# Probabilities of query blocks 8 to 14 transposed through DRAM and VectorE instead of TensorE

## The reference

```
energy = (x @ Wq) @ (x @ Wk).T          # per batch, 2048 x 2048
energy = where(pad | causal, -inf, energy)
z = softmax(energy / sqrt(32)) @ (x @ Wv)
```

## Time and profile before

| | |
|---|---|
| time, median of 3 runs | 1645.36 us (1645.16 to 1645.95) |
| the profiled execution: its time, its span | 1649.54 us, 1647.7 us |
| busy: PE, DVE, ACT, POOL | 98%, 53%, 35%, 22% of the span |
| mean granted TensorE clock | 0.994 of 2.4 GHz |
| transposes of probabilities on TensorE (L970) | 272, of which 168 are of blocks 8 to 14 in both batches |
| DMA | 130.87 MB, 79 GB/s on average |

### The profile page before, as it was taken

How to read it: one execution, slowest core, us unless ns; L and a number is a source line. 1 busy time by engine, 2 the same in 40 slices (tenths; PEclk the granted TensorE clock), 3 DMA queues, 4 the chain that set the end, 5 groups by cost and what they waited for, 6 DMA issues and landing times.

```text
span 1647.7 us, 20596 instructions
## 1 busy us (share of the span) xinstructions
PE 1610.7 (98%) x7538; PEld 1323.5 (80%) x7538; DVE 876.6 (53%) x1784; ACT 572.6 (35%) x990; POOL 363.9 (22%) x562
## 2 busy tenths in 40 slices
PE   8999999999999999899999899999999999999999
PEld 6887888877788888677777688888888888888887
DVE  6757544477664444688888966333333332423311
ACT  5432121134222212466666544232323232333322
POOL 1212100022220000288888911000000000000000
PEclk9999999999999999799999999999999999999999
DMA  6302110131221104456664354111212111121100
GB/s 213 101 27 96 45 52 26 39 110 58 72 74 34 52 26 142 135 140 171 157 178 163 112 157 126 64 39 56 47 52 50 54 39 64 39 64 32 46 0 26
DMA packets 177161, 130.87 MB, mean 79 GB/s; under 512 B 121073, under 2 KB 121073, under 8 KB 176907
## 3 DMA queue, kind: packets, MB, share of 16 engines
q1 hardware_dynamic: 175264, 126.10, 25.9%
q10 hardware_dynamic: 1797, 3.46, 0.6%
HBM read 87.34 MB, written 42.18 MB: 79 GB/s over the span
## 4 chain that ended last, share of the span: by engine, by line
PE 85%; DVE 6%; ACT 4%; issue 2%; POOL 2%; DMA 0%; DVEq 0%; SPq 0%; ACTq 0%; POOLq 0%
PE banks L760 82%; PE banks L970 2%; ACT plain L1318 2%; DVE split L1697 1%; ACT split L1154 1%; PE banks L770 1%; DVE plain L2068 1%; ACT plain L1328 1%; DVE tile_x L2075 0%; DVE plain L2058 0%; DMA plain<-in_L_xattn_Wk 0%; POOL split L1572 0%; DVE plain L1836 0%; DVE split_q L1697 0%; POOL split L1579 0%
## 5 line engine op out<-in xcount | busy, mean ns | idle before, releaser
L760 PE MATMUL banks<-split_q,split 128*128 128x512 f32 x2328 | 565.8, 393 | 4.9 <-POOL split L1572 3.0
L760 PE MATMUL banks<-split 128*128 128x512 f32 (+5 forms) x2304 | 543.0, 385 | 8.3 <-DVE split L1697 5.9
L760 PEld LDWEIGHTS banks<-split_q,split 128*128 128x128 f32 x2328 | 434.1, 188 | 98.7 <-POOL split L1572 4.0
L760 PEld LDWEIGHTS banks<-split 128*128 128x128 f32 (+3 forms) x2304 | 414.8, 185 | 103.9 <-issue 8.2
L760 PE MATMUL banks<-split,split_q 128*128 128x512 f32 (+3 forms) x1728 | 393.2, 380 | 7.2 <-DVE split_q L1697 4.1
L760 PEld LDWEIGHTS banks<-split,split_q 128*128 128x128 f32 x1728 | 308.4, 189 | 60.3 <-DVE split_q L1697 4.9
L2216 DVE TENSOR_TENSOR split<-plain,split 128x512 fp32r<-128x512 f32 x128 | 88.5, 692 | 386.8 <-ACT split L1473 386.7
L1467 ACT ACTIVATE plain<-banks,small 128x512 f32<-128x512 f32 x128 | 88.3, 690 | 402.4 <-PE banks L760 402.4
L1697 DVE TENSOR_TENSOR split<-banks,split 128x512 fp32r<-128x512 f32 (+5 forms) x232 | 146.1, 637 | 149.4 <-ACT split L1154 149.1
L1154 ACT ACTIVATE split<-banks 128x512 fp32r<-128x512 f32 (+5 forms) x232 | 124.0, 555 | 244.5 <-PE banks L970 190.9
L1506 POOL TENSOR_TENSOR small<-small 128x1 f32<-128x1 f32 x64 | 13.1, 204 | 475.6 <-DVE small L1733 475.4
(11 more groups left out here) (157 smaller groups left out, 1265.3 us busy)
## 6 DMA issues: line engine op xcount, KB each, us to landing
plain<-in_x SPq DMA_DIRECT2D x64, 256.0 KB, 2.7
xo_scratch<-plain SPq DMA_DIRECT2D x32, 256.0 KB, 2.3
x_scratch<-plain SPq DMA_DIRECT2D x32, 256.0 KB, 2.0
plain<-x_scratch SPq DMA_DIRECT2D x32, 256.0 KB, 3.0
tile_x<-xo_scratch SPq DMA_DIRECT2D x32, 256.0 KB, 3.2
xg_scratch<-tile_x SPq DMA_DIRECT2D x32, 256.0 KB, 2.1
out<-plain SPq DMA_DIRECT2D x32, 256.0 KB, 2.1
plain<-xg_scratch SPq DMA_DIRECT2D x7, 1024.0 KB, 5.5
```

The lines of the kernel that those rows point to most:

```text
L760: mm = nc.tensor.matmul(out, left(c, l), right(c, r), start=start and c == 0 and (l, r) == PASSES[0], stop=stop and c == chunks - 1 and (l ...
```

## The change

Blocks 8 to 14 are `turned`. When X(i) is done, SP stores the row of probabilities to `p_dram`, chunk by chunk (`store_p`). Each chunk is then loaded back into the same place of `Srow` by four DMAs (`load_p`), so that the 32x32 squares of every 128x128 tile stand where the transposed tile wants them. SP issues the loads of chunks 0 and 2. A new step O(i) has ScalarE issue those of chunks 1 and 3, after a wait for the store of the same chunk. A new step I(i,c) has VectorE wait for the four loads and transpose the chunk in 32x32 squares into bank 2 or 3; TensorE has no part in T of these blocks. The list of steps is another one for these blocks.

```
+        if turned(i) and n1 > n0:
+            g = i // 4 + 1
+            order += [("Q", g, 0), end[0], ("Q", g, 1), end[1], ("I", i, 0), ("I", i, 1), ("Q", g, 2), ("T", i, 0),
+                      ("Q", g, 3), ("T", i, 1), ("V", i, 0), ("I", i, 2), ("S", i + 1, 0), ("T", i, 2)]
+            order += [("S", i + 1, c) for c in range(1, n1)]
+            order += [("X", i + 1, 0), ("O", i + 1, 0), ("V", i, 1), ("V", i, 2)]
+        elif turned(i):
+            order += [end[0], ("S", i + 1, 0), ("S", i + 1, 1), ("I", i, 0), ("T", i, 0), ("S", i + 1, 2), ("I", i, 1),
+                      ("T", i, 1), end[1]]
+            order += [("S", i + 1, 3)] if n0 > 3 else []
+            order += [("X", i + 1, 0), ("I", i, 2), ("V", i, 0), ("T", i, 2), ("O", i + 1, 0)]
+            order += [("I", i, 3), ("V", i, 1), ("T", i, 3)] if n0 > 3 else [("V", i, 1)]
+            order += [("V", i, c) for c in range(2, n0)]
...
-            order += [("S", i + 1, n0), ("X", i + 1, 0)]
+            order += [("S", i + 1, n0), ("X", i + 1, 0), ("O", i + 1, 0)]
...
+        def load_p(eng, b, i, c):
+            at, w = c * 512, width_of(i, c)
+            eng.wait_ge(p_out[c], squares_in(b, i, c) * 16)
+            squares_of = p_dram[c, 0:P * w].rearrange("(q s c i r) -> i s c q r", q=QB, s=32, i=QB, r=32)
+            for n in range(QB):
+                eng.dma_start(Srow[32 * n:32 * n + 32, i % 2, at:at + w].rearrange(
+                    "p (c q r) -> p c q r", q=QB, r=32), squares_of[n]).then_inc(p_in[c], 16)
...
+                def store_p(i, c):
+                    n, at, w = squares_in(b, i, c), c * 512, width_of(i, c)
+                    if n > 1:
+                        sp.wait_ge(p_in[c], (n - 1) * QB * 16)
+                    sp.dma_start(p_dram[c, 0:P * w].rearrange("(p n) -> p n", n=w), Srow[:, i % 2, at:at + w]).then_inc(p_out[c], 16)
...
                     sp.dma_start(x1_dram[b * S + i * P:b * S + (i + 1) * P, :], U[:, i % 2]).then_inc(
                         x1_out[i % 2], 16)
+                    if turned(i + 2):
+                        sp.wait_ge(p_ready, b * NB + i + 2 + 1)
+                        for c in range(chunks_of(i + 2)):
+                            store_p(i + 2, c)
+                        for c in range(0, chunks_of(i + 2), 2):
+                            load_p(sp, b, i + 2, c)
...
-                    elif kind == "T":
+                    elif kind == "T" and not turned(i):
...
+                    elif kind == "O" and turned(i):
+                        for n in range(1, chunks_of(i), 2):
+                            load_p(act, b, i, n)
...
+                    elif kind == "I":
+                        n, at, w = TURNS["p", b, i, c], c * 512, width_of(i, c)
+                        dve.wait_ge(p_in[c], squares_in(b, i, c) * QB * 16)
+                        dve.wait_ge(tp_free, n + 1)
+                        nc.vector.transpose(PS[:, 2 + n % 2, 0:w], Srow[:, i % 2, at:at + w]).then_inc(tp_full, 1)
```

More of the change, by code:

```diff
@@ L89, with turned, squares_in @@
 T_BEFORE = [sum(chunks_of(j) for j in range(i)) for i in range(NB + 1)]
+def turned(i):
+    return 8 <= i < NB - 1
+def squares_in(b, i, c):
+    return sum(turned(j) and c < chunks_of(j) for j in range(NB)) * b + sum(
+        turned(j) and c < chunks_of(j) for j in range(i + 1))
 def attention_order(b):
@@ L109, in attention_order @@
         end = [(kind, i - 1, 0) for kind in "AB"]
-        if n1 > n0:
+        if turned(i) and n1 > n0:
[11 more added lines that the diff above has]
+            order += [("V", i, c) for c in range(2, n0)]
+        elif n1 > n0:
             g = i // 4 + 1
@@ L169, in turns_of_attention @@
         for kind, i, c in ORDERS[b]:
-            if kind == "T":
+            if kind == ("I" if turned(i) else "T"):
                 order.append(("p", b, i, c))
@@ L255, in build @@
         xg_dram = nc.dram_tensor("xg_scratch", (B * S, E), F32, kind="Internal").ap()
+        p_dram = nc.dram_tensor("p_scratch", (C, P * 512), F32, kind="Internal").ap()
         h_dram = nc.dram_tensor("h_scratch", (TILE, E), F32, kind="Internal").ap()
@@ L438, in build @@
         h_out, hb_in = sem("h_out"), sem("hb_in")
+        p_out, p_in = [sem(f"p_out_{c}") for c in range(C)], [sem(f"p_in_{c}") for c in range(C)]
         block = ctx.enter_context(nc.Block())
@@ L966, in _ @@
                             pe.wait_ge(p_ready, b * NB + i + 1)
+                        if c == 0 and turned(i - 1):
+                            pe.wait_ge(tp_full, n)
                         pe.wait_ge(tp_free, n + 1)
```

## The result

The changed kernel takes 1685.4 us (median of 4 runs, 1684.0 to 1691.1) where the kernel before takes 1645.7: ratio 1.0237, 95% interval 1.0209 to 1.0265. It is 39.7 us slower; 33.7 were forecast, and the time lies in the range. The profiled execution's span is 1689.3 us against 1647.7, 41.6 us more.

A forecast was written before the change was run, and what follows sets the result against it. TensorE, busy for 98% of the span, was taken to bound the kernel. Saved transposes, waits and low clock summed to -19.7 + 47.8 + 5.6 = +33.7 us, a median of 1679 us, range 1654 to 1698.

The forecast's parts named there:

- What is taken away: TensorE's transposes in blocks 8 to 14: 168 tiles in two batches at 0.118 us, 19.7 us saved.
- The walk: Steps followed through stretches 8 to 14: TensorE waits before V, 23.9 us a batch, 47.8 in two.
- the slower pace of two queues: SP and ScalarE loading at once: ScalarE's eight issues take up to 1.3 us more, 5 us over four stretches; upper end only.
- The clock: TensorE's clock falls behind the 4.4 to 4.7 us gaps in four stretches, 1.4 us each: 5.6 us.
- The sum: Whole kernel: -19.7 + 47.8 + 5.6 = +33.7 us, median 1679 us.
- The first (O doesn't hold ScalarE): Load issues on ScalarE slip past its other work or take next to nothing: +9.9 us, 1655; chance 0.14.
- The second (every stretch pays for the clock): More gaps in changed stretches cost clock, 19.6 us, and the two queues crowd, 5: +52.7 us, 1698; chance 0.14.
- The third (hand-overs stay ahead): ScalarE and VectorE stay ahead of TensorE, so the 168 tiles are simply saved: 1625.7 us; chance 0.07.
- the loads are not late: Loads by squares in the changed stretches could land 6 us later without a price.

The follow-up runs named there:

- experiment 10: Changed kernel with only blocks 12 to 14 turned, I and T of chunks 0 and 1 a step earlier, B behind X, O last: 1637.5 us, 0.9941 of before.
- experiment 1: Changed kernel with only step O(i+1) moved behind T(i,3) in four-chunk stretches: 1656.7 us, 1.0065 of the kernel before.
- experiment 3: Changed kernel with O in its place but reduced to its waits for the stores, SP issuing every load: 1661.0 us, 1.0091 of before.
- experiment 2: Changed kernel with all loads issued by SP and none by ScalarE: 1661.2 us, 1.0089 of the kernel before.
- experiment 4: Changed kernel with O issuing only the four loads of chunk 1, SP the rest: 1670.3 us, 1.0144 of the kernel before.
- experiment 9: Changed kernel with I and T of chunks 0 and 1 a step earlier, B behind X, O still ahead of T(i,3): 1675.6 us, 1.0182 of before.

## Why the prediction was right

**What is taken away.** Forecast 0.118 us a tile. Experiment 10 gives 0.11. From the start of V(7,0) to T(15,0) of the first batch takes 146.3 us before and 150.4 in experiment 1, +4.2, with 13.0 us of waits; so 84 tiles saved 8.8 there, 0.105 each. In experiment 10 the same time is 4.9 and 4.7 us shorter than before in the two batches, 9.6 in all. The term was 19.7 and is 17.6 by the first of these, 18.8 by the median of experiment 10 and 19.2 by its trace: right, or slightly high.

**The walk.** The places were right in all seven stretches, and the sum, 23.9 a batch, came out as 25.3. The wait before the last V of stretches 12 and 13 was under-sized: 5.1 and 6.3 for 4.4 and 4.7. ScalarE reached its first issue 2.8 us after X (2.7 forecast), but the eight issues, put at 5.2 us, took 5.57 in stretch 12 and 6.50 in stretch 13, and 5.56 and 5.60 in those of the second batch. The term was too small by 0.4 us, and in one stretch by 1.3. These are ScalarE's issues in stretch 13 of the first and of the second batch, and SP's in stretch 13 of experiment 3 (ns least/median/most):

```profile
L527 ACTq DMA_DIRECT2D plain<-p_scratch x8: 564/651/1543, 326.3 to 332.2; - x8
L527 ACTq DMA_DIRECT2D plain<-p_scratch x8: 564/647/916, 656.7 to 661.6; - x8
L527 SPq DMA_DIRECT2D plain<-p_scratch x16: 562/636/1467, 317.7 to 328.6; - x16
```

So 0.9 of the 1.3 us is a single issue of 1.54, and one of 1.47 is there with a single queue too. It is not the slower pace of two queues that I had kept for the upper end; that would have given 1.3 us in all four stretches. In the traces of all the experiments each of the 45 load issues over 0.95 us overlaps a packet of the instruction queue; the others take at most 0.93. That the packet is the cause is not tried.

The Trainium skill states that DMAs of both queues run on the same 16 engines and interleave there (DMA: Bandwidth & Descriptors, "Issuing engines are not separate DMA queues"). The trace agrees, but in the landing: the loads land 2.8 us after their issue at the median with both queues, 2.4 with SP alone (experiment 2).

Against that the wait before V(13,2) was 1.7 for 2.25.

**The clock.** Forecast 5.6 us, measured 10.6 if the first batch stands for both. Behind the long waits V(12,3), S(14), V(13,3) and S(15) took 0.8, 1.6, 1.4 and 1.5 us more than in experiment 1, where the clock stayed up: 5.3 a batch. I had taken the price of one short fall; here the low clock lasted twice as long. The four falls came where they were forecast. A fifth came in the second batch, behind a wait of only 2.3 us before V(12,2), and experiment 2 has falls behind waits of 2.0: that gaps shorter than 2.47 us bring none, the reason for taking four falls, did not hold.

**The sum.** 2 x 25.3 + 10.6 - 17.6 = +43.6 against the profiled +41.6 and the median's +39.7. Doubling the first batch says a little too much. From V(7,0) to T(15,0) the first batch grew by 21.6 us, which 25.3 + 5.3 - 8.8 gives, but the second by 19.1: from start to start its waits before V(11,0), V(12,2) and V(13,3) were 0.9, 0.6 and 0.9 us shorter. Both make 40.7 of the profiled 41.6. The waits and above all the clock were too small, the saving slightly too large; the forecast of +33.7 is short by 6.

**The rivals.** The first (O doesn't hold ScalarE) falls by rows 326.31 and 332.91 of the timeline and by experiments 1, 4 and 9. The second (every stretch pays for the clock) falls too: of the five falls that the attention shows, four stand behind the long waits, and the crowding of the two queues did not come in its size, as told above. The third (hand-overs stay ahead) is false for this order, and true for blocks 12 to 14 in experiment 10. That the loads are not late held: VectorE has no wait for `p_scratch` in the changed kernel.

## What to carry to other kernels

A DMA issue on a compute engine is work of that engine: here 0.66 us each at the median and up to 1.5, and in an in-order queue it is paid by whatever stands behind it, so it belongs behind the last step that somebody waits for. Work taken off the bounding engine is a gain only if its replacement is ready as early; walk one period of the loop on every engine in its own order, and the first wait shows where the order has to change. The same move, with the order mended and applied only where the next stage hides the transfer, turned +2.4% into -0.6%.

## What was not expected of the hardware

**A two-input VectorE operation doubled beside GpSimd.** In stretch 12 of the changed kernel:

```profile
290.19 1.30 POOL L1590 TENSOR_TENSOR plain<-plain 128x512 f32<-128x512 f32 x1 [8.76 <-DMA plain<-in_x]
290.37 1.67 DVE L1794 SCALAR_TENSOR_TENSOR plain<-plain,small 128x512 f32<-128x512 f32 x1
```

L1794 takes 0.75 at the median. SP's loads had made the `x` block late, so that GpSimd's addition fell on B, and the wait before V(12,2) is 2.86 us, where experiment 1 has 1.95. It is no effect of the change by itself; line L1739 of the kernel before, the same operation, has it too (ns least/median/most):

```profile
L1739 DVE SCALAR_TENSOR_TENSOR plain<-plain,small x32: 750/752/1878, 127.0 to 690.1; 128x512 f32<-128x512 f32 x32
```

The trace of the kernel before has 64 such operations (L1737 and L1739). The 46 that overlap no addition of GpSimd take 0.74 to 0.75 us. The nine that begin while one runs take 0.92 to 1.77, and each ends 0.55 us after the addition does. In the changed kernel ten of twelve do the same; the other two begin in its last 0.15 us and take 0.74. So VectorE's operation does not run slowly, it stands until GpSimd's is over, and moving a transfer can shift one onto the other.

**One load issue in 40 takes 1.0 to 1.7 us,** over all the experiments, in place of 0.64 to 0.66, and each of these stands beside a 16 KB packet of the instruction queue. The one store that landed late, 4.4 us for 192 KB (experiment 3), has such a packet beside it too.

**The clock stayed low for 6.8 us** in the first batch, after 4.8 and 6.0 us of idling, while waits of 1 to 2 us brought no fall in the first batch of experiment 1 and falls of 3.4 us in experiment 2. A wait of 2.86 us in the changed kernel brought none, one of 2.32 did. What tells these apart no run here shows.
